# First layer of a two-layer conv, attention and mixture-of-experts kernel: matmuls of ones ahead of the norm, half steps between the logits' halves, and one store on another queue

## What is computed

```
x = x + conv_moe(group_norm(x, 32 groups))    # 8 experts of width 512, top 2, GELU, and a shared gated FFN
t = x.reshape(4, 256, 192)
t = t + attention(layer_norm(t))              # 12 heads of 16, softmax, mask, softmax
t = t + moe(layer_norm(t))                    # 16 experts of width 384, top 2, SiLU, and a shared gated FFN

conv_moe(h): scores = softmax(h @ gate_w.T); top 2, weights renormalised
             out = sum over experts e of w_e * (gelu(h @ fc1[e].T + b1[e]) @ fc2[e].T + b2[e])
             shared = (gelu(h @ w1.T + b) * (h @ w3.T + b)) @ w2.T + b
group_norm:  mean and variance over one image and the 6 channels of a group
```

## Time and profile before

| what | value |
|---|---|
| median of 3 runs | 442.93 us (442.3 to 443.37) |
| the profiled execution, its own time | 443.52 us |
| its span, first to last instruction | 441.6 us |
| PE busy | 403.3 us (91%) |
| DVE, ACT, POOL busy | 262.2, 186.4, 128.2 us |
| DMA | 39.41 MB |

### The profile page before, as it was taken

One profiled execution on the slowest core, in us unless ns is written; L12 is line 12 of the kernel. 1 busy time (PEld: TensorE's weight loads), 2 busy tenths in 40 slices (PEclk: granted clock), 3 DMA queues, 4 the chain that ended last, 5 costly groups with the idle time before them and its releaser, 6 DMA issues.

```text
span 441.6 us, 7990 instructions
## 1 busy us (share of the span) xinstructions
PE 403.3 (91%) x2303; PEld 298.9 (68%) x2304; DVE 262.2 (59%) x673; ACT 186.4 (42%) x463; POOL 128.2 (29%) x137
## 2 busy tenths in 40 slices
PE   0899998999999999988889877999899999999995
PEld 0755455776776888866757665845678887878884
DVE  3526424222222187789898975474597777777734
ACT  1123231222222124898787873331444455444410
POOL 4300224555554100000000000001265555555630
PEclk9999999999999999999999999999999999999999
DMA  8999201111100487000000079790011111110007
GB/s 225 267 295 340 57 24 37 39 46 46 42 24 10 135 264 308 1 1 1 1 2 1 1 179 242 176 249 14 16 38 44 34 35 39 50 44 23 0 0 214
DMA packets 20888, 39.41 MB, mean 89 GB/s; under 512 B 5711, under 2 KB 14965, under 8 KB 20418
## 3 DMA queue, kind: packets, MB, share of 16 engines
q1 hardware_dynamic: 11362, 29.66, 23.6%
q0 software_dynamic: 5280, 6.85, 5.4%
q10 hardware_dynamic: 4224, 2.62, 2.1%
HBM read 36.21 MB, written 7.93 MB: 100 GB/s over the span
## 4 chain that ended last, share of the span: by engine, by line
PE 81%; ACT 6%; DMA 5%; DVE 5%; issue 2%; ACTq 0%; DVEq 0%; SPq 0%; POOLq 0%
PE bank L1371 13%; PE bank L1282 12%; PE bank L1344 9%; PE bank L1349 9%; PE bank L1544 5%; PE bank L1360 5%; PE bank L1498 4%; DMA w_first<-y_rows 3%; PE bank L1560 3%; PE bank L1326 3%; PE bank L1355 2%; PE bank L1354 2%; PE bank L1268 2%; PE bank L1592 2%; ACT xn_t L755 2%
## 5 line engine op out<-in xcount | busy, mean ns | idle before, releaser
L549 POOL DMA_INDIRECT rows<-xn_rows,slot_tok x56 | 59.7, 1067 | 88.7 <-DVE slot_tok L935 52.5
L557 POOL DMA_INDIRECT y_rows<-y,slot_row x54 | 55.4, 1026 | 78.7 <-DVE y L1003 41.6
L1371 PE MATMUL bank<-w_second,hid_t 128*128 x370 | 69.5, 327 | 2.8 <-DVE hid_t L988 2.8
L1371 PEld LDWEIGHTS bank<-w_second,hid_t 128*128 128x128 f32 x370 | 58.8, 190 | 3.7 <-issue 3.5
L1349 PE MATMUL bank<-w_first,rows_t 128*128 x124 | 45.3, 488 | 0.4 <-issue 0.4
L1005 DVE TENSOR_TENSOR y<-bank,w_second 128x192 f32<-128x192 f32 x23 | 8.2, 357 | 60.2 <-PE bank L1371 60.2
L988 DVE COPY hid_t<-bank 128x384 f32<-128x384 f32 (+1 forms) x54 | 33.0, 611 | 18.0 <-PE bank L1360 12.9
L1344 PE MATMUL bank<-w_first,rows_t 96*128 (+1 forms) x92 | 43.4, 594 | 0.1
L654 ACT ACTIVATE act_h<-bank 128x512 f32<-128x512 f32 x23 | 13.7, 597 | 65.0 <-PE bank L1344 65.0
L597 POOL COPY act_h<-o_inv 128x256 f32<-128x256 f32 x12 | 4.8, 400 | 122.9 <-DVE o_inv L1169 122.9
L659 ACT ACTIVATE act_g<-bank 128x384 f32<-128x384 f32 x31 | 15.2, 491 | 48.1 <-PE bank L1355 48.1
(11 more groups left out here) (198 smaller groups left out, 790.2 us busy)
## 6 DMA issues: line engine op xcount, KB each, us to landing
w_first<-in_gate_up SPq DMA_DIRECT2D x16, 384.0 KB, 6.9
w_second<-in_down SPq DMA_DIRECT2D x1, 4608.0 KB, 17.6
w_first<-in_fc SPq DMA_DIRECT2D x1, 3072.0 KB
w_second<-in_fc SPq DMA_DIRECT2D x1, 3072.0 KB, 28.2
w_first<-in_gate_up_rest SPq DMA_DIRECT2D x16, 192.0 KB, 7.5
rows<-xn_rows,slot_tok POOLq DMA_INDIRECT x56, 2.7
y_rows<-y,slot_row POOLq DMA_INDIRECT x54, 2.3
w_first<-in_x_t SPq DMA_DIRECT2D x2, 384.0 KB, 4.8
```

What stands on the lines that cost most here:

```text
L549: pool.indirect_dma_start(rows[b % 2][:, 0:ROW[L.l]], None, xn_rows[L.l], bass.IndirectOffsetOnAxis(slot_tok[:, b:b + 1].bitcast(U32), 0), ...
L557: pool.indirect_dma_start(y_rows[L.l], bass.IndirectOffsetOnAxis(slot_row[:, b:b + 1].bitcast(U32), 0), y[b % 2][:], None, bounds_check=TO ...
L1371: ins = pe.matmul(bank[:, 1, 0:C], hid_t[:, tile(ic)], w(P, ic * C, C), start=(ic == 0), stop=(ic == L.IC - 1))
```

## The change

It does four things.

1. TensorE waits for POOL's first constant and then issues six matmuls of `ones` by `ones` with 512 moving columns into bank 1, which nobody reads, before the wait for the statistics; one more with 256 columns between the two group averages, and four with 256 columns after the second.
2. The one stage `"logits"` becomes `"logits0"` and `"logits1"`, each of four tiles, which wait for 4 and for 8 of the instructions that write `xn_t`.
3. The shared steps `(0, 0)` and `(0, 1)` move: one stands before `"logits0"`, one between the halves.
4. The store of the normed rows moves from SP's queue to ACT's. There it stands behind ACT's four copies to `xn_tok` and ahead of its next GELU; SP's wait stays.

```
         plan = {
-            0: (["logits", (0, 0), (0, 1), "rows", (1, 0), "count", (1, 1), "rank", (2, 0), "expert", (2, 1), (3, 0),
+            0: ([(0, 0), "logits0", (0, 1), "logits1", "rows", (1, 0), "count", (1, 1), "rank", (2, 0), "expert", (2, 1), (3, 0),
                  (3, 1), "slots", (4, 0), (4, 1), (5, 0), (5, 1), (6, 0), (6, 1), "first rows", (7, 0), (7, 1)],
...
             sp.wait_ge(tp_out, NT // 2)
-            sp.dma_start(by_tile(xn_rows[0]), xn_tok[:]).then_inc(xn_stored, 16)
             sp.dma_start(wqkv[:, 0:NCH * QKC * P], d["wqk"].rearrange("p k c m -> p (k c m)")).then_inc(s_qkvw, 16)
...
                 if s == 0:
                     act_norm_transposes(act, 0, range(NT // 2))
+                    act.wait_ge(tp_out, NT // 2)
+                    act.dma_start(by_tile(xn_rows[0]), xn_tok[:]).then_inc(xn_stored, 16)
...
+            def warm_up(n, columns):
+                for _ in range(n):
+                    pe.matmul(bank[:, 1, 0:columns], ones[:], bc(ones[:], 1, [P, columns // P, P]),
+                              start=True, stop=True)
+
+            pe.wait_ge(pool_c, 1)
+            warm_up(6, 4 * P)
             pe.wait_ge(s_const, 16)
             pe.wait_ge(chan_ready, NCH * IMAGES)
             pe.matmul(bank[0:CH, 0, 0:NCH * IMAGES], gavg, chan_mv[:, :, 0], start=True, stop=True
                       ).then_inc(gmean_ps, 1)
+            warm_up(1, 2 * P)
             pe.wait_ge(dev_ready, 1)
             pe.matmul(bank[0:CH, 0, 64:64 + NCH * IMAGES], gavg, chan_dev[:], start=True, stop=True
                       ).then_inc(gvar_ps, 1)
+            warm_up(4, 2 * P)
             pe.wait_ge(filled, 1)
...
-                elif s == "logits":
-
+                elif s in ("logits0", "logits1"):
+                    half = int(s[-1])
                     pe.wait_ge(s_gate0, 16)
-                    for j in range(NT):
-                        if j % 2 == 0:
-                            pe.wait_ge(xn_t_ready, NCH * (j // 2 + 1))
+                    pe.wait_ge(xn_t_ready, NCH * IMAGES // 2 * (half + 1))
+                    for j in range(half * NT // 2, (half + 1) * NT // 2):
                         logits(L, j)
```

## The result

The changed kernel takes 447.48 us in the median of 4 executions (445.6 to 451.7), the kernel before 442.96: ratio 1.0107, interval 1.0076 to 1.0138. It's slower by 1.1%, where 436.8 was forecast and the range ended at 439.6. All four executions lost clock on TensorE (means over the span 0.976 to 0.989, the kernel before 0.999 or more in most of its own).

What follows compares the result with a forecast made beforehand. PE, 81% of the chain, bounds the kernel, its early matmuls at 1.2 GHz. Gains 3.30 + 3.74 + 0.36 less 0.64 give 6.76 us; 443.52 - 6.76 = 436.76, so 436.8, range 435.8 to 439.6.

Steps and rivals of the forecast that it cites:

- PE's program up to (1,0): First layer's shared steps, logits and transposes: at 2.4 GHz, (1,0) begins at 21.51 us where it began at 28.27, 6.76 earlier.
- the fillers' end: Unread matmuls before the norm: 12 PE instructions from about 1.0 us, halving in duration, ending between 8.3 and 9.4 us.
- At `count` PE didn't wait for DVE: Behind (1,0): DVE's `before_ready` at 22.83, needed at 23.26, a margin of 0.4 us where it was 7.
- the store is hidden: Normed rows' store on ACT's queue: lands at 35.8 us, rows by 41.8, wanted at 45.7; 3.9 us of slack, no cost.
- The attention's loads: On SP's queue: issued 6.8 us sooner without the store ahead, read only in the expert blocks and later; cost nothing.
- Rival 2: First rows late: store lands no sooner than 41.3 us, 1.4 lost, 438.2; each further us costs one more; chance 0.08.
- "Its lengths unchanged": Rest of the trace behind the first rows: everything 6.8 us earlier, at the same clock and with the same lengths.
- whether the clock stays up: PE from about 9 to 12.8 us, with only fillers: they keep it busy some 2.5 us of 3.8, holding 2.4 GHz.
- The rule of the Trainium skill: Store's queue: all issuing queues' DMAs share 16 engines; several only save sequencer time; literally, the store lands at 41.3 as now.

Runs made afterwards that it cites:

- loads held back: Changed kernel, store still on ACT's queue, but SP issues the attention's loads only when the store has landed: 444.71 us.
- store on SP's queue: Changed kernel with only the store of the normed rows put back on SP's queue, behind fc2 and its bias: 445.53 us.
- fillers in the wait: Changed kernel plus six unread matmuls of 512 columns on PE directly ahead of the first layer's first rows: 448.1 us.

## Why the prediction was wrong

- **Right: PE's program up to (1,0).** Forecast 6.76 us earlier, measured 6.75. The logits took the 1.7 of the forecast and the fillers' end at 8.98 lies within 8.3 to 9.4. That the sum agrees to 0.01 is luck: (0,0) began 0.3 us sooner than forecast (12.50 against 12.8), and the two steps took 0.3 more (1.96 and 1.82 against 1.75 each). At `count` PE didn't wait for DVE, as forecast.
- **The step that failed: the store is hidden.** It took the second layer's 13.7 us for a store on ACT's queue and got a landing at 35.8 and 3.9 us of slack. It landed at 48.4, 26.3 us after its issue, and PE sat idle for 6.5 us. The row was from another load: what counts is not the queue, but what stands in the other queue and in what packets. The forecast said "in its own queue it needn't wait for `fc2` to drain"; the packet counts show that it waits for `fc2` and for everything behind it.
- **The attention's loads** were costed at nothing, because nobody reads them early. They have no reader, but they have packets: with them out of the way the store landed at 41.7 (loads held back), and when they were under way beside the gather it took 5.8 us (store on SP's queue) and 6.8 (loads held back).
- **Rival 2 was the right place with part of the price.** It gave 438.2 for a landing at 41.3 and one us for each further one: 445.3 at 48.4, less 2.1 since the gather then took 2.8 and not 4.9, so 443.2. Its wait, 1.4 + 7.1 - 2.1 = 6.4 us, is the 6.5 that was measured. What it lacked is the clock: it fell in the idle time, for another 2.9 us, and again in the second layer, for 1.7. Its range ended at 440, which left out a landing as late as 48.
- **"Its lengths unchanged" for the rest of the trace failed as well.** From 9 to 12.8 us, where the forecast asked whether the clock stays up, it did in the profile of every kernel with the fillers. Beyond, it was taken for granted from one execution. The same second layer's logits lost the clock in three profiled executions of other kernels, and the first layer's logits and transposes in the profiles of four. One execution shows that a stretch can keep the clock, not that it will. The kernel before kept it nearly everywhere (mean 0.999 or more in 75 of the 85 executions timed beside the experiments); why it's steadier there than with the fillers wasn't settled.
- The rule of the Trainium skill weighed in the forecast (Trainium Kernel Development and Optimization, Key Constraints), that issuing from several queues only saves the sequencer's time, is too mild by these runs: the same store landed 6.5 us later on ACT's queue than on SP's (48.4 and 41.9), although it was issued at nearly the same time (22.1 and 21.7).

## What to carry to other kernels

Before you move a small-packet transfer to a queue of its own, look at what the other queue holds at that moment, and in what packets. The transfer is done when each of its packets has had a turn, and the size of the other queue's packets sets how long the turns take: here 132 of them in 5 us beside packets of 15 KB, 383 beside 3.3 KB, 832 with the other queue nearly empty. In order in the other queue the transfer may be done sooner. When PE gets faster ahead of a transfer, work out the transfer's landing under the new traffic, with loads that come up sooner counted in, and put it at the place in the queue where it's needed. Price a wait of several us on PE twice, as idle time and as slow matmuls behind it, and look at several executions' clocks before you count on a stretch to keep it.

## What the runs showed of the hardware

- A 768 KB store of 768-byte rows took 26.3 us on its own queue beside a full one, 20.2 in order behind what was left of 3 MB of weights, and 10.4 or less ahead of them.
- A gather of 128 rows took 2.8 us with the other queues empty, 5.8 and 6.8 among the attention's loads, and 9.0 to 9.7 among the experts' weights.
- The clock fell in or behind 6.5, 4.6 and 3.4 us of idle PE, and in one profile behind 1.54; behind 1.24 and 2.16 us (fillers in the wait) it stayed up. Once down at 21.4 us, it stayed down until 38 with PE busy throughout, nearly all of it with 512-column matmuls, and with single steps between logits it was still down at 42 us, 29 us after the start of the first of them; in contrast, in every profile it rose while the twelve unread matmuls at the start ran (they took 7.0 to 8.3 us, where the lower level alone gives 10.2).
